# An expert stage that begins from a first table of 27 batches, with the last four batches routed between its tiles

## What is computed

```python
h = _layernorm(x) * (1 + ca) + sa
x = x + ga * attention(h, wq, wk, wv, wo)      # 8 heads, width 128, causal, rms norm and rope on q and k
h = _layernorm(x) * (1 + cb) + sb
scores = softmax(h @ Wr + br)                  # 8 experts
_, top_idx = top_k(scores, 2)
weights = softmax(where(chosen, scores, -inf))
hid = gelu(h @ W1[e] + b1[e])                  # 128 -> 512
out = hid @ W2[e] + b2[e]                      # 512 -> 128
x = x + gb * sum over the two chosen e of weights[e] * out[e]
```

## Time and profile before

| | |
|---|---|
| runs (3) | 1233.54, 1234.32, 1234.9 us; median 1234.32 |
| the profiled execution | 1234.39 us, its span 1232.5 us |
| mean granted clock of TensorE | 0.955 of full |
| busy of the span | PE 86%, PEld 65%, DVE 75%, ACT 77%, POOL 76% |
| attention block | 0 to about 940 us |
| expert tiles | about 940 to 1184 us |
| mixing | about 1184 to 1232.5 us |

### The profile page before, as it was taken

The page is one execution under the profiler, slowest core; times in us unless marked ns, Lnnn a source line. Parts: engine busy times, 40 slices in busy tenths (PEclk is TensorE's granted clock), DMA queues, the critical chain, the costliest instruction groups (busy, mean ns, idle before and its releaser), DMA issues. The chain is left out here.

```text
span 1232.5 us, 30653 instructions
## 1 busy us (share of the span) xinstructions
PE 1055.4 (86%) x7439; PEld 802.9 (65%) x7439; DVE 928.7 (75%) x2613; ACT 954.5 (77%) x3428; POOL 932.7 (76%) x1296
## 2 busy tenths in 40 slices
PE   4689999999999999999999999999933999999900
PEld 2268777777777777777777777777821555568800
DVE  2887888877888887888888788887533777778745
ACT  3798888888888888888887888888612999999723
POOL 2877778888888888888888888888662566666844
PEclk9999999999999999999999999999965999999955
DMA  8300000000000000000000000000004432221166
GB/s 269 107 26 4 6 4 16 17 13 11 14 11 12 16 15 12 11 14 11 14 16 14 12 12 13 11 16 17 16 24 136 118 99 92 88 87 46 41 216 197
DMA packets 50770, 57.73 MB, mean 47 GB/s; under 512 B 7868, under 2 KB 38703, under 8 KB 50644
## 3 DMA queue, kind: packets, MB, share of 16 engines
q1 hardware_dynamic: 32916, 34.84, 9.5%
q0 software_dynamic: 8704, 16.87, 3.9%
q10 hardware_dynamic: 9024, 4.72, 1.3%
HBM read 33.21 MB, written 24.23 MB: 47 GB/s over the span
## 5 line engine op out<-in xcount | busy, mean ns | idle before, releaser
L469 POOL TENSOR_TENSOR roped<-roped,rope_b 128x512 f32<-128x512 f32 x256 | 334.2, 1306 | 85.1 <-DVE rope_b L923 80.3
L654 ACT ACTIVATE squares<-unit 128x128 f32<-128x128 f32 x1024 | 271.7, 292 | 18.7 <-PE unit L1066 17.9
L654 ACT ACTIVATION_READ_ACCUMULATOR squares<-unit 128x1 f32 x1024 | 225.5, 223 | 0.0
L1342 POOL DMA_INDIRECT y_rows<-y_out,place_y x144 | 154.1, 1070 | 93.1 <-DVE y_out L1456 54.8
L909 DVE TENSOR_TENSOR roped<-unit,cos_sb 128x512 f32<-128x512 f32 x256 | 173.4, 677 | 61.0 <-ACT squares L654 60.2
L621 ACT ACTIVATE probs<-scores,rr 128x256 f32<-128x256 f32 x256 | 123.9, 484 | 100.4 <-PE scores L1102 73.7
L923 DVE TENSOR_TENSOR rope_b<-unit,sin_sb 128x512 f32<-128x512 f32 x256 | 173.4, 677 | 0.0
L499 POOL DMA_INDIRECT x_rows<-rows,place x128 | 126.0, 985 | 33.7 <-issue 33.0
L1141 PEld LDWEIGHTS unit<-ident,roped 128*128 128x128 f32 x1024 | 117.9, 141 | 43.0 <-POOL roped L469 16.3
L1141 PE MATMUL unit<-ident,roped 128*128 128x128 f32 x1024 | 135.2, 275 | 9.7 <-ACT k_t L673 4.4
L877 DVE SCALAR_TENSOR_TENSOR acc<-pv,den,acc 128x128 f32<-128x128 f32 x448 | 135.5, 337 | 0.3
(11 more groups left out here) (213 smaller groups left out, 2965.5 us busy)
## 6 DMA issues: line engine op xcount, KB each, us to landing
back<-y_rows SPq DMA_DIRECT2D x16, 512.0 KB, 5.5
tile_x<-x_rows SPq DMA_DIRECT2D x25, 258.0 KB, 2.7
x_all<-in_L_attn_x SPq DMA_DIRECT2D x32, 128.0 KB, 2.1
out_x<-sums ACTq DMA_DIRECT2D x16, 256.0 KB, 4.4
tile_x<-x_rows SPq DMA_DIRECT2D x22, 129.0 KB, 2.1
y_rows<-y_out,place_y POOLq DMA_INDIRECT x144, 2.3
k_t<-in_L_ffn_W SPq DMA_DIRECT2D x2, 1024.0 KB, 9.8
ga_b<-mod_dram SPq DMA_DIRECT2D x32, 64.0 KB, 2.8
```

The source lines that it names most:

```text
L469: pool.tensor_tensor(out=roped[parity][:, u, heads], in0=roped[parity][:, u, heads], in1=rope_b[:, u % 2, heads], op=ALU.add).then_inc(S[" ...
L654: nc.scalar.activation(squares[:, c * D:(c + 1) * D], UN[0][:, c * D:(c + 1) * D], ACT.Square, accum_out=ssq[parity][:, u * H + c:u * H + ...
L1342: pool.indirect_dma_start(out=y_rows, out_offset=bass.IndirectOffsetOnAxis(ap=place_y[at][:, s:s + 1], axis=0), in_=y_out[at][:, s, :], in ...
```

## The change

1. The attention block ends with step 33. RT and ST are live for batches 0 to 27 only; N2 for 0 to 29.
2. In step 32 PE sums the counts of the first 27 batches, and DVE makes the first 20 entries of the table from them (14 instructions, between its heads 3 to 7): big tiles that are full already. SP loads tiles 0 to 2 at the end of the attention block, into buffers that lie in `rope_b`.
3. In the expert block, POOL begins with the residual of batch 31, DVE with its statistics. Then the last four batches (1,024 tokens) are routed together, by pieces at the head of the steps n of the tile loop: ACT in steps 0, 2, 5, 6, 8, 9, DVE in 1, 4, 6, 7, 8, 9 and 11 to 15, PE in 2, 3, 5, 7, 10, POOL in 11 (16 indirect DMAs). The weights come from tanh in place of exp and reciprocal.
4. The rest of the table (27 entries) is made by DVE in steps 11 to 14 (32 instructions), SP writes the filler rows in step 12, and tile 20 is the first that waits for them.
5. The second of the two down banks is given to the routing (`RB`); down products wait for `y_cols` of the tile before.

In this cut of the diff the `@block` lines name the engine: sync is SP, gpsimd POOL, scalar ACT, vector DVE, tensor PE. The first sync and the first vector part are of the attention block, all others of the expert block.

```diff
+    LATE = 4
+    LAST = NB - LATE
+    TABLED = NB - LATE - 1
+    NEARLY = -(-(K * TABLED * T - E * (BIG - 1)) // BIG)
...
-                return [0 <= n + d < NB for d in (2, 1, 0, -1, -2, -3, -4, -5, -6)]
+                return [0 <= n + d < (LAST if d < -4 else NB) for d in (2, 1, 0, -1, -2, -3, -4, -5, -6)]
...
-            for n in range(NB - 2, NB + 6):
+            for n in range(NB - 2, NB + 2):
                 body(n // 2, n % 2, live(n))
...
         @block.sync
...
-            fill_tails(sp, 0)
+            sp.wait_ge(S["add_done"], H * NB)
+            sp.wait_ge(S["table_step"], EARLY_STEPS)
+            for k in range(2):
+                sp.wait_ge(S[f"scattered{k}"], 16 * TT * K * ((TABLED - 1 - k) // 2 + 1))
+            for i in range(EARLY):
+                fetch(i)
+                for row, cols in first_rows(i):
+                    sp.dma_start(early_x[i], x_rows[bass.ds(row, BIG), :].rearrange("(p s) c -> p s c", p=P))\
+                        .then_inc(S[f"tile_in{i}"], 16)
...
         @block.vector
...
+                    if isinstance(n, int) and n == NB:
+                        if h == 3:
+                            early_counts()
...
+                        elif h == 7:
+                            early_table()
...
         @block.sync
...
+                if n == 12:
+                    sp.wait_ge(S["table_step"], COUNT_STEPS)
+                    for expert in range(E):
+                        end = sp.value_load(counts_i[0:1, expert:expert + 1], min_val=0, max_val=NTOK)
+                        sp.dma_start(x_rows[bass.ds(end + expert * REGION, TILE), :]
...
+                    if i == NEARLY:
+                        sp.wait_ge(S["late_scattered"], 16 * LT * K)
+                        sp.wait_ge(S["filled"], 16 * (SPARE + E))
...
         @block.gpsimd
...
+            pool.tensor_tensor(out=acc[mine][:, :, :], in0=acc[mine][:, :, :],
+                               in1=ga_b[mine][:, :].rearrange("p (o m) -> p o m", o=1).to_broadcast([P, TT, M]),
+                               op=ALU.mult).then_inc(S["x2_done"], 1)
...
+            pool.tensor_tensor(out=x_all[:, TT * b:TT * NB, :], in0=x_all[:, TT * b:TT * NB, :],
+                               in1=acc[mine][:, :, :], op=ALU.add).then_inc(S["x2_done"], 1)
...
+            def late_scatter():
+                pool.wait_ge(S["late_rows"], LATE)
+                pool.wait_ge(S["late_tagged"], LATE)
+                pool.wait_ge(S["late_place"], 4)
+                for g in range(LT):
+                    for j in range(K):
+                        at = place_l[:, g * K + j:g * K + j + 1]
+                        pool.indirect_dma_start(
+                            out=x_rows, out_offset=bass.IndirectOffsetOnAxis(ap=at, axis=0),
+                            in_=rows_l[:, g // TT, j, g % TT, :], in_offset=None).then_inc(S["late_scattered"], 16)
             def body(n, live):
+                if n == 11:
+                    late_scatter()
...
         @block.scalar
...
+                if n == 0:
+                    late_roots()
+                elif n == 2:
+                    late_h2()
+                elif n == 5:
+                    late_exp()
+                elif n == 6:
+                    late_rows(0)
+                elif n == 8:
+                    late_rows(1)
+                elif n == 9:
+                    late_tanh()
...
         @block.vector
...
+            late_stats()
...
+                if n == 1:
+                    late_normal()
+                elif n == 4:
+                    late_top()
+                elif n == 6:
+                    late_score()
+                elif n == 7:
+                    late_best()
+                elif n == 8:
+                    late_which()
+                elif n == 9:
+                    late_choice()
+                elif n == 11:
+                    late_places()
+                    all_counts()
+                elif n == 12:
+                    all_ends()
+                elif n == 13:
+                    all_steps()
+                elif n == 14:
+                    all_experts()
+                    all_table()
+                elif n == 15:
+                    late_weights()
+                    fetch(NBIG)
...
         @block.tensor
...
+                if n == 2:
+                    late_turn()
+                elif n == 3:
+                    late_logits()
+                elif n == 5:
+                    late_back(0)
+                elif n == 7:
+                    late_back(1)
+                elif n == 10:
+                    late_prefix()
...
                     wait(pe, "hid_split", 2 * (i + 1))
+                    wait(pe, "y_cols_done", parts_to(i))
                     for one, at in columns_of(i):
-                        dst = DN[other][:, at]
+                        dst = DN[:, at]
```

More of the change, by code:

```diff
@@ L156, in adaln_block @@
         bst2 = sb("bst2", [P, TT, 6])
-        xn2 = sb("xn2", [P, TT, M])
-        rows = [sb(f"rows{k}", [P, K, TT, RW]) for k in range(2)]
-        h2_t = sb("h2_t", [P, T])
+        mod_t = sb("mod_t", [P, 4, NB])
         wr_sb = sb("wr_sb", [P, E])
@@ new lines, in adaln_block @@
+        ln_eps = sb("ln_eps", [P, TT])
+        minus_half = sb("minus_half", [P, NCH])
+        three_halves = sb("three_halves", [P, NCH])
+        half_vx = sb("half_vx", [P, NCH])
+        ln_vx = sb("ln_vx", [P, NCH])
+        guess = sb("guess", [P, NCH])
+        correction = sb("correction", [P, NCH])
+        rr = [sb(f"rr{k}", [P, NCH]) for k in range(2)]
+        xn2 = sb("xn2", [P, TT, M])
+        rows = [sb(f"rows{k}", [P, K, TT, RW]) for k in range(2)]
+        h2_t = sb("h2_t", [P, T])
@@ L219, in adaln_block @@
+        chosen = sb("chosen", [P, TT, E], BF16)
+        place_e = sb("place_e", [P, TT, E])
+        place_k = sb("place_k", [P, TT * K, E])
+        place_f = sb("place_f", [P, TT * K])
+        place = [sb(f"place{k}", [P, TT * K], I32) for k in range(2)]
+        behind = squares[:, 0:NENT * E].rearrange("p (i e) -> p i e", e=E)
         UN = [ps(f"unit{k}", [P, 2 * 512]) for k in range(2)]
@@ L704, in body @@
                         wait(act, "h2t_done", b + 1)
-                        wait(act, "rt_done", b)
-                        wait(act, "h2_back", b)
-                        nc.scalar.activation(h2_t[:, :], UN[1][:, 0:T], ACT.Identity,
+                        late = isinstance(b, int) and b >= LAST
+                        if not late:
+                            wait(act, "rt_done", b)
+                            wait(act, "h2_back", b)
+                        nc.scalar.activation(h2_late[:, b - LAST, :] if late else h2_t[:, :], UN[1][:, 0:T],
+                                             ACT.Identity,
                                              scale=mod_t[:, 3, bass.ds(b, 1)],
@@ L753, in body @@
+            def body(half, parity, live, heads=H):
                 n = 2 * half + parity
@@ L889, in small @@
                             route(n - 5, k)
-                for h in range(H):
+                for h in range(heads):
                     w, u, bank = 2 * NU * n + h, h // 2, h % 2
@@ L1024, in _ @@
[L1024 to L1028 removed]
+            body(NB // 2 + 1, 0, [False] * 5 + [True] + [False] * 3, 1)
@@ L1182, in body @@
                         ins.then_inc(S["h2t_done"], 1)
+                    if isinstance(n, int) and n == NB and h == 2:
+                        wait(pe, "counted", TABLED)
+                        wait(pe, "rope_done", 2 * NU * NB)
+                        nc.tensor.matmul(UN[0][:, 0:E], ones_bf[:, :], counts[TABLED % 2][:, :], start=True, stop=True)\
+                            .then_inc(S["count_done"], 1)
                     if RT and h == 1:
@@ new lines, in _, with late_top @@
+            logits = RB[:, 0:LT * E].rearrange("p (g e) -> p g e", e=E)
+            def late_top():
+                dve.wait_ge(S["late_logits"], 1)
+                for g in range(LT):
+                    nc.vector.max(top_ll[:, g, :], logits[:, g, :]).then_inc(S["late_max"], 1)
+                dve.wait_ge(S["late_max"], LT)
+                nc.vector.tensor_tensor(out=less_l[:, :, :], in0=logits, in1=top_ll[:, :, 0:1].to_broadcast([P, LT, E]),
+                                        op=ALU.subtract).then_inc(S["late_less"], 1)
```

573 lines of the change are left out of this document (402 added, 171 removed).

## The result

The changed kernel takes 1226.78 us (median of 4 runs, 1225.96 to 1227.44) against 1234.61 (4 runs, 1233.54 to 1235.75): ratio 0.9936, 95% interval 0.9919 to 0.9953. It is faster by 0.6%, where 2.0% was forecast, and outside the forecast's range (1197 to 1221). The profiled execution has a span of 1225.6 us against 1232.5, 6.9 less where the sum said 24.7 less. On a second chip the same kernel gave 0.9932 (0.9920 to 0.9945).

The account below looks back on a forecast made before the run. PE was taken as the bound, with some 50 us standing between attention and expert stage. -43 + 2.8 + 1.3 + 10.8 + 2.4 + 1 = -24.7 us from 1234.39 gave 1209.7, stated as 1209.5, range 1197 to 1221.

Parts of the forecast that it names:

- Seam, -43: Between attention and expert stage: the first up product comes at 903.5 in place of 946.54 us, 43 us earlier.
- Clock at the seam, equal: PE's half clock around the seam, returning 4.9 us after the first up product, is the same in both kernels.
- PE +2.8: Before step 11, PE's added transposes, logits products and prefix products all count, costing 2.8 us.
- ACT +1.3: Added ACT work and two table loads in the expert stage make y_cols late in steps 5 and 6; PE stands 1.3 us.
- DVE just fits: DVE's added routing instructions stand at 1 to 2.1 us per step and fit up to step 13; step 14 (2.7) would not.
- POOL +10.8: Sixteen late scatters in step 11 delay tile 9's stored rows; DVE waits in step 14 and PE stands 10.8 us around step 15.
- half clock +2.4: After its stop around step 15 PE resumes at half clock for 4.9 us, costing 2.4 us.
- tail +1: POOL gains some 0.35 us a step on PE; the lag left behind the last tile adds 1 us (bounds 0 and 6).
- second rival: Expert stage: POOL never recovers and its backlog from the late scatters stays whole at the end; 1220 us taken, chance 0.2.
- The mixing stage is not touched: The mixing stage at the kernel's end is unchanged, so no time was put on it.
- The first rival: Expert stage: POOL takes the late scatters in its idle time, so stall, half clock and tail go; 1195.5 us, chance 0.13.
- the slower case: Routing waits in steps 3 to 15 keep PE at 1.2 GHz, steps taking 12.1 us; eight such steps give 1258, chance 0.03.

Follow-up runs that it names:

- e9: Changed kernel with nine more POOL drains, at the seam, start of the experts, ahead of several tiles' scatters and behind the last; 1270.68 us on a slow chip (before 1274.5).
- e13: Kernel before with two more POOL drains, at 112 scatters in the attention block's tail and ahead of tile 28's scatters; 1245.67 us (before 1236.27).
- e14: Changed kernel with two more POOL drains, at 104 scatters in the attention block's tail and ahead of tile 24's scatters; 1227.84 us (before 1236.27).
- e17: Changed kernel without POOL's drain at the seam, with it at the end; 1216.75 us, ratio to before 0.9846.
- e6: Changed kernel without POOL's drain at either block's end and with ten tables place_y in place of six; 1212.29 us, ratio to before 0.9805.
- e15: Changed kernel without POOL's drain at either block's end; 1210.87 us, ratio to before 0.9787.
- e18: Changed kernel with POOL's drain at the seam and without it at the end; 1219.26 us, ratio to before 0.9859.
- e3: Changed kernel with ten tables place_y in place of six, drains kept; 1259.48 us on a slow chip, ratio to before 0.9962.
- e10: Changed kernel with ten tables place_y in place of six, drains kept, on the second slow chip; 1268.81 us, ratio to before 0.9954.

## Why the prediction was right or wrong, point by point

- **Seam, -43.** Measured -35.1. Every step of it held but one: the last scatter at 895.14 (894.53 before), DVE's last sum 1.7 us later than before (it ends at 898.12, within POOL's drain), tiles loaded, first up product 4.4 us behind the release (5.0 said). The failed step is "POOL's drain takes 1.38 us": a row of before taken as the price of an instruction, when it was the price of 16 scatters behind a clearing. With 112 it is 9.22 (e9, e13 and e14 show it by count, e17 by leaving it out). The condition named for being wrong, a first up product after 910, is what happened.
- **Clock at the seam, equal.** Half clock from 901.8 to 915.5, 4 us behind the first up product: as said.
- **PE +2.8, ACT +1.3.** Together 4.1; measured 6.7 up to tile 8. The logits products took 2.3 us, not 1.0: 16 narrow f32 passes at 0.12, when I had four full transposes at 0.11 each as the bound for nine of them and left out the second pass. The half clock behind them, +1.7, was in no term. The rest, from tile 1's scatters to tile 8's, came to 2.3 where 2.7 of the sum lay (eight transposes 0.9, the prefix 0.5, ACT 1.3); of these the prefix products took 0.3. ACT ran the load and the next ACTIVATE 1.29 and 1.30 us apart and began the load 0.02 us behind the hid_hi ahead of it: nothing of the further 1.38 us of the Trainium skill (ScalarE: Activation LUTs, What ACT_TABLE_LOAD costs) shows in these rows.
- **DVE just fits.** The longest wait of PE for DVE between 915 and 1006 us is 1.1 us: held. In step 14, where 2.7 us too many were said, DVE's x_lo starts 1006.50 - 1002.29 = 4.2 us behind PE's transposes, before 1013.79 - 1012.50 = 1.3, so it is 2.9 us late.
- **POOL +10.8, half clock +2.4, tail +1: 14.2.** The wait is at the place forecast. Its length is in part luck: by the terms DVE would have waited from 1032.7 to 1046.8, 14.1 us, and it came 2.9 us late itself. PE, for which the 10.8 was meant, stood 9.2 us in two pieces (8.05 and 1.18) and lost 17.49 - 6.05 = 11.4 with the half clock, where 13.2 was said ("longer idle than at the old seam", in the prediction, is not so; there PE had next to nothing to do for some 50 us). From tile 8's scatters to the last 16.6 are measured (-28.4 to -11.8). The size was nearly right and the logic was not: e6 takes the wait and the half clock away and nothing moves, because POOL's own lag is the longer chain. The failed step here is "POOL gains some 0.35 us on PE in a step": it had 5.7 us for POOL's four scatters, and they take 4 x (1.19 + 0.30) = 6.0. So the lag stays nearly whole, and PE's stop lies inside it. The sign named for the second rival, POOL never waiting for DVE behind the scatters, is what came. So the second rival (0.2) had the mechanism, with its scatter of 1.87 us in each tile, and was the worse in size: 22.4 - 1.0 = 21.4, since some tiles pass without a long scatter and POOL made up 5.3 of the 21.9 us that it lost in step 11. The long scatter at 1085.96 and the stretched ones of before end 0.84 to 0.86 us behind the end of the first hid_lo instruction under which they begin. The Trainium skill (SBUF — State Buffer, Who interferes with whom) has GpSimd short of the shared ports for its descriptors under some DVE instructions, but of a tensor_tensor with two SBUF inputs, which hid_lo is, it says that it holds up GpSimd's reads and, as an inference, not the writing of descriptors. The trace agrees with a hold-up and does not tell which of the two it is. No run took hid_lo away, so the cause of the stretch is argued, not shown.
- **"The mixing stage is not touched", 0.** Its work was not. The drain behind it was 4.9 us longer. This is a failed step of the same kind as the seam's: a term put at nothing because nothing was changed there.
- **The sum.** 7.9 (seam) + 2.6 + 2.4 + 4.9 = 17.8 us short in spans. 12.8 of them are two drains. Without any drain (e15) the span is 1207.5, where the sum had put it (1207.8); that this closes so well is partly chance, since POOL's and PE's terms were 5 us too small and leaving the drains out saves more than they had grown.
- The first rival (late scatters hidden) and the slower case did not come; the half clock in the expert stage was once 3.4 and once 10 us long.

## What to carry to other kernels

A drain at a block's end is not a constant: read what its engine has issued since the last one, and when a change moves DMAs across the block's end or changes their number, price the drain again; where every DMA is awaited by semaphore, it can be left out (here 1.3 to 1.5% of the changed kernel's time). When an engine takes over a block of work in the middle of a stage that it almost fills, ask first whether it ever catches up: the stalls that it hands to others are then cover for its own lag, and removing them gives nothing, as the ten tables did. A price of an instruction taken from one row holds for the state in which that row was recorded; write the state beside it.

## What the runs showed of the hardware

- POOL's drain: 0.082 us for each scatter of 128 rows since the last drain (8 to 112 of them; 0.5 us more right behind a scatter), 0.03 us with none (e9). In the attention block a 114th scatter without a drain pauses 1.9 to 2.2 us once, and the drain behind 128 is 1.4 us. Behind 144 to 272 the end's drain is 4.0 or 8.9 us; what decides is open.
- A scatter that starts under DVE's hid_lo takes up to 1.9 us in place of 0.97, and ends 0.84 to 0.86 us behind that instruction's end.
- Sixteen narrow f32 passes (128x8) on PE take 1.95 us, 0.12 each; 1.86 us of weight loads (PEld) stand beside them.
- PE's granted clock can fall to half with PE busy throughout (0.57 in 932 to 936), in some kernels and not in others (e18, e3, e10) that are alike up to there.
